# Two state-space layers: stacked float32r step-size products, a later small projection, and step sizes of the first layer grouped by function

## What is computed

```python
xp = jnp.einsum('bld,rd->blr', x, x_proj_w)           # 512 -> 16 + 16 + 16
dt = jax.nn.softplus(jnp.einsum('blr,dr->bld', dt_in, dt_proj_w) + dt_proj_b)
h = dA_t * h + dBx_t                                  # scan over 64 tokens
y = jnp.moveaxis(ys, 0, 1) + D * x
```

```python
u, gate = jnp.split(hidden_states @ W_in.T, 2, axis=-1)        # 1024 each
u = jax.nn.silu(conv4(u) + conv_b)
dt, Bm, Cm = jnp.split(u @ Wx.T, [R, R + N], axis=-1)          # 32 + 16 + 16, each rms-normalised
delta = jax.nn.softplus(dt @ Wdt.T + dt_bias)                  # 32 -> 1024
state = dA * state + (d_t * u_t)[..., None] * B_t[:, None, :]
y = (ys + u * D_param) * jax.nn.silu(gate);  return y @ W_out.T
```

## Time and profile before

| | us |
|---|---|
| median of three runs | 3992.61 (3990.76 to 3992.87) |
| the profiled execution | 3989.96 |
| its span | 3988.2 |
| busy: TensorE | 3646.0 (91%) |
| busy: VectorE | 2273.9 (57%) |
| busy: ScalarE | 1538.5 (39%) |
| busy: GpSimd | 1382.3 (35%) |
| mean granted clock of TensorE | 0.958 |
| first layer, first step-size product to scan stage | 1085.36 to 1115.41 |
| second layer, first stage | 3269.87 to 3409 |
| second layer, step sizes, group 0 | 3409.30 to 3444.32 |
| second layer, step sizes, group 1 | 3638.63 to 3672.61 |

### The profile page before, as it was taken

One profiled execution on the slowest core, in us unless ns is written; L12 is line 12 of the kernel. 1 busy time (PEld: TensorE's weight loads), 2 busy tenths in 40 slices (PEclk: granted clock), 3 DMA queues, 4 the chain that ended last, 5 costly groups with the idle time before them and its releaser, 6 DMA issues. The chain is left out here.

```text
span 3988.2 us, 74956 instructions
## 1 busy us (share of the span) xinstructions
PE 3646.0 (91%) x32236; PEld 2435.1 (61%) x32236; DVE 2273.9 (57%) x2567; ACT 1538.5 (39%) x2213; POOL 1382.3 (35%) x887
## 2 busy tenths in 40 slices
PE   6999999999768589999999999999999999686888
PEld 4555655555233456887877777788888747233334
DVE  3666666665299832444445544444445326597972
ACT  2555555555277312222222222222222103575740
POOL 3344444441189211111111111111111004496971
PEclk8999999999789899999999999999999999697999
DMA  6455555552222032111111111111111220221220
GB/s 210 126 139 141 146 142 139 141 148 52 86 67 81 22 144 68 40 48 40 39 31 47 30 48 40 38 40 40 48 40 44 78 79 1 78 90 53 90 69 21
DMA packets 225841, 301.66 MB, mean 76 GB/s; under 512 B 65328, under 2 KB 171760, under 8 KB 224224
## 3 DMA queue, kind: packets, MB, share of 16 engines
q1 hardware_dynamic: 225512, 296.88, 25.1%
HBM read 243.25 MB, written 53.10 MB: 74 GB/s over the span
## 5 line engine op out<-in xcount | busy, mean ns | idle before, releaser
L1743 POOL TENSOR_TENSOR D_ctx_lo<-D_ctx_raw,D_ctx_hi 128x1904 fp32r<-128x1904 f32 x64 | 256.1, 4003 | 1291.2 <-ACT D_ctx_hi L1737 1291.2
L762 DVE TENSOR_REDUCE A_mxc<-A_psX 128x2 f32<-128x768 f32 (+2 forms) x512 | 485.6, 985 | 207.1 <-PE A_psX L792 206.1
L1058 ACT ACTIVATE A_probs<-A_psE 128x1024 f32<-128x1024 f32 (+1 forms) x416 | 426.2, 1025 | 315.0 <-PE A_psE L1091 309.8
L1761 ACT ACTIVATE D_V<-D_psY 119x384 f32<-119x384 f32 x224 | 109.8, 490 | 842.8 <-PE D_psY L1828 842.8
L2059 ACT ACTIVATE D_probs<-D_psE 119x2048 f32<-119x2048 f32 x112 | 210.5, 1879 | 415.0 <-PE D_psE L2186 415.0
L1777 DVE TENSOR_REDUCE D_mxc<-D_psE 128x4 f32<-128x1904 f32 (+1 forms) x128 | 242.2, 1893 | 190.7 <-PE D_psE L1847 190.5
L1828 PE MATMUL D_psY<-D_wv_hi,D_ctx_hi 128*119 128x384 f32 (+1 forms) x896 | 314.7, 351 | 16.5 <-DVE D_K_lo L1772 9.0
L2104 DVE TENSOR_TENSOR D_acc<-D_acc,D_probs 119x1024 f32<-119x1024 f32 x96 | 117.6, 1225 | 353.4 <-ACT D_probs L2059 353.4
L2200 PE MATMUL D_psO<-D_probs,D_V 119*32 119x256 f32 (+1 forms) x5376 | 313.3, 381 | 0.0
L1828 PE MATMUL D_psY<-D_wv_hi,D_ctx_lo 128*119 128x384 f32 (+1 forms) x896 | 302.1, 337 | 0.0
L1828 PE MATMUL D_psY<-D_wv_lo,D_ctx_hi 128*119 128x384 f32 (+1 forms) x896 | 301.9, 337 | 0.0
(11 more groups left out here) (360 smaller groups left out, 7802.4 us busy)
## 6 DMA issues: line engine op xcount, KB each, us to landing
D_ctx_raw<-in_ctx SPq DMA_DIRECT2D x48, 952.0 KB, 5.2
A_land<-in_ctx SPq DMA_DIRECT2D x32, 768.0 KB, 6.0
A_land<-in_ctx SPq DMA_DIRECT2D x16, 1024.0 KB, 5.6
E_Bn<-bc_scratch SPq DMA_DIRECT2D x64, 256.0 KB, 3.6
E_Cn<-bc_scratch SPq DMA_DIRECT2D x64, 256.0 KB, 3.4
k_scratch<-A_Khl SPq DMA_DIRECT2D x32, 384.0 KB, 5.2
A_Kst<-k_scratch SPq DMA_DIRECT2D x64, 192.0 KB, 3.5
A_land<-in_ctx SPq DMA_DIRECT2D x16, 642.0 KB, 4.4
```

Of the source, the lines that this page charges most:

```text
L762: nc.vector.tensor_reduce(mxc[:, u % 4, :, u // 4], psX[:, x % 2, :, 0:w], axis=AX_X, op=ALU.max).then_inc(x_free, 1)
L1058: nc.scalar.activation(probs[0:KW[k], n % NPR, :, :].rearrange("p h q -> p (h q)"), psE[0:KW[k], :], ACT.Exp, scale=HD ** -0.5).then_inc(e ...
L1743: nc.gpsimd.tensor_tensor(ctx_lo[c][:, :, 0:w], ctx_raw[c][:, :, 0:w], ctx_hi[c][:, :, 0:w].bitcast(F32), ALU.subtract).then_inc(lo_done[c ...
```

## The change

- *Step sizes of the second layer.* z becomes one float32r product over 128 rows. PT is made on 128 partitions: wx, lnw and share hold the dt part three times, at rows 0, 64 and 96. ScalarE copies PT to the float32r tile PS in two halves, VectorE subtracts to get the low part in rows 96 to 127. The weights ws have in the same way high part, zeros, low part, high part. PT itself moves to a fixed place, and eu shares the space of duT.
- *Small projection two chunks behind*: x_product(c - 2) from c = 2 on, and three at the end. The last chunk's U is made by VectorE.
- *An early Ln* of the tiny eps behind the squares.
- *First layer*: the second layer's pattern: Abs from PSUM for all four chunks in ORDER, then Exp, then Ln; transposes of xpT behind the first product; du of chunks 1 and 3 on GpSimd; duT copied by ScalarE.

```diff
@@ l0_mamba, TensorE
+                    pe.wait_ge(x_out, 2)
+                    for k, c in enumerate(ORDER):
+                        if k == CN - 1:
+                            pe.wait_ge(b_out, 1)
                         for half in range(2):
-                            pe.wait_ge(x_out, 2)
-                            nc.tensor.matmul(ps[:, 2 * c + half, :], wdt[:, bass.ts(c, P)],
-                                             xpT[0:R, bass.ts(half, 512)], start=True, stop=True).then_inc(z_full, 1)
...
+                        last.then_inc(z_full, 1)
+                        if k == 0:
+                            for t in range(NPAIR):
+                                last = nc.tensor.transpose(ps[:, 2 * ORDER[-1], RN * t:RN * t + RN],
+                                                           xpT[:, bass.ts(t, P)], consts["ident"][0:RN, 0:RN])
+                            last.then_inc(b_full, 1)
@@ l0_mamba, GpSimd
                     ffn_weights.prepare(pool)
+                    for k, c in enumerate(ORDER):
+                        if c not in B_ON_PE:
+                            pool.wait_ge(delta_made, k + 1)
+                            nc.gpsimd.tensor_tensor(du[:, c, :], delta[:, c, :], XnT[:, c, :], ALU.mult)
@@ l1_mamba, loads
-            nc.sync.dma_start(wx[:, :, :], a["L1_attn_Wx"]).then_inc(wx_in, 16)
+            nc.sync.dma_start(wx[:, :, 0:RN], a["L1_attn_Wx"]).then_inc(wx_in, 16)
+            for row in COPIES[1:]:
+                nc.sync.dma_start(wx[:, :, row:row + R], a["L1_attn_Wx"][:, :, 0:R]).then_inc(wx_in, 16)
+                nc.sync.dma_start(lnw[row:row + R, :], a["L1_attn_dt_ln_w"].rearrange("o n -> n o")).then_inc(wx_in, 16)
...
+            for row in COPIES:
+                nc.sync.dma_start(wdt[row:row + R, :], a["L1_attn_Wdt"]).then_inc(wdt_in, 16)
@@ l1_mamba, TensorE
-                        if c == 1:
-                            pe.wait_ge(wx_in, 64)
-                        x_product(c - 1)
+                        if c == 2:
+                            pe.wait_ge(wx_in, 16 * 8)
+                        if c >= 2:
+                            x_product(c - 2)
+                    x_product(C - 2)
                     x_product(C - 1)
@@ l1_mamba, ScalarE
                         norm.out(act, t)
+                    act.wait_ge(wdt_in, 48)
+                    act.wait_ge(wdt_zero, 1)
+                    nc.scalar.activation(ws[:, :], wdt[:, :], ACT.Copy).then_inc(ws_hi, 1)
                     act.wait_ge(padded, 1)
...
                     act.wait_ge(eps_made, 1)
+                    nc.scalar.activation(early[:, :], eps[:, :], ACT.Ln)
                     act.wait_ge(ms_full, 2)
...
+                    for half in range(2):
+                        act.wait_ge(pt_made, half + 1)
+                        nc.scalar.activation(PS[:, bass.ts(half, 512)], PT[:, bass.ts(half, 512)], ACT.Copy
+                                             ).then_inc(ps_hi, 1)
@@ l1_mamba, GpSimd
+                    pool.wait_ge(ws_hi, 1)
+                    link(nc.gpsimd.tensor_tensor(ws[RN:RN + R, :], wdt[RN:RN + R, :], ws[RN:RN + R, :].bitcast(F32),
+                                                 ALU.subtract))
-                    for c in range(C):
+                    for c in range(C - 1):
@@ l1_mamba, VectorE
+                    dve.wait_ge(sig_u, C)
+                    nc.vector.tensor_tensor(U[:, C - 1, :], U[:, C - 1, :], eu[:, (C - 1) % 2, :], ALU.mult
+                                            ).then_inc(silu_last, 1)
...
-                    nc.vector.scalar_tensor_tensor(PT[:, :], psx[0:RN, :], lnw[:, 0:1], rms, ALU.mult, ALU.mult)
+                    for half in range(2):
+                        nc.vector.scalar_tensor_tensor(PT[:, bass.ts(half, 512)], psx[:, bass.ts(half, 512)],
+                                                       lnw[:, 0:1], rms[:, bass.ts(half, 512)], ALU.mult, ALU.mult
+                                                       ).then_inc(pt_made, 1)
+                    for half in range(2):
+                        dve.wait_ge(ps_hi, half + 1)
+                        rest = slice(RN + R, P)
+                        nc.vector.tensor_tensor(PS[rest, bass.ts(half, 512)], PT[rest, bass.ts(half, 512)],
+                                                PS[rest, bass.ts(half, 512)].bitcast(F32), ALU.subtract)
@@ l1_mamba, TensorE, step sizes
-                                                            wdt[:, bass.ts(CG * g + c, P)],
-                                                            PT[0:R, bass.ts(half, 512)], start=True, stop=True)
+                                                            ws[:, bass.ts(CG * g + c, P)],
+                                                            PS[:, bass.ts(half, 512)], start=True, stop=True)
```

More of the change, by code:

```diff
@@ new lines, in _ @@
+                    for k, c in enumerate(ORDER):
+                        dve.wait_ge(z_made, k + 1)
+                        dve.wait_ge(ln_made, k + 1)
+                        nc.vector.tensor_tensor(delta[:, c, :], delta[:, c, :], du[:, c, :], ALU.add
+                                                ).then_inc(delta_made, 1)
+                        if c in B_ON_PE:
+                            dve.wait_ge(delta_made, k + 1)
+                            nc.vector.tensor_tensor(du[:, c, :], delta[:, c, :], XnT[:, c, :], ALU.mult
+                                                    ).then_inc(du_made, 1)
@@ L2368, in x_product @@
                     def x_product(c):
-                        pe.wait_ge(silu_u, c + 1)
+                        if c < C - 1:
+                            pe.wait_ge(silu_u, c + 1)
+                        else:
+                            pe.wait_ge(silu_last, 1)
                         for half in range(2):
-                            last = nc.tensor.matmul(psx[0:RN, bass.ts(half, 512)], wx[:, c, :],
+                            last = nc.tensor.matmul(psx[:, bass.ts(half, 512)], wx[:, c, :],
                                                     U[:, c, bass.ts(half, 512)], start=(c == 0), stop=(c == C - 1))
@@ L2397, in _ @@
                         pe.wait_ge(sq_made, half + 1)
-                        nc.tensor.matmul(ps[0:RN, 1, bass.ts(half, 512)], share[:, :], sq[:, bass.ts(half, 512)],
+                        nc.tensor.matmul(ps[:, 1, bass.ts(half, 512)], share[:, :], sq[:, bass.ts(half, 512)],
                                          start=True, stop=True).then_inc(ms_full, 1)
@@ L2462, in _ @@
                     nc.gpsimd.memset(eps[:, :], RMS_EPS).then_inc(eps_made, 1)
+                    pool.wait_ge(eps_made, 1)
+                    nc.gpsimd.memset(wdt[R:RN, :], 0.0).then_inc(wdt_zero, 1)
+                    pool.wait_ge(wdt_zero, 1)
                     norm.power_of(pool, range(0, NPAIR // 2))
@@ L2468, in _ @@
                     link(nc.gpsimd.memset(share[0:R, :], 0.0))
-                    link(nc.gpsimd.memset(share[0:R, 0:R], 1.0 / R))
+                    for row in COPIES:
+                        link(nc.gpsimd.memset(share[0:R, row:row + R], 1.0 / R))
                     link(nc.gpsimd.memset(share[R:RN, :], 0.0))
```

104 lines of the change are left out of this document (53 added, 51 removed).

## The result

| | before | after |
|---|---|---|
| median, us (runs) | 3992.74 (4) | 3964.47 (4) |
| lowest to highest | 3990.76 to 3994.68 | 3962.47 to 3968.65 |
| profiled execution / its span | 3989.96 / 3988.2 | 3962.47 / 3960.7 |
| mean granted clock | 0.958 | 0.963 |

The account below looks back on a forecast made before the run. TensorE, busy for 91% of the span, was taken to bound the kernel. Terms -9.8 - 9.7 - 4.3 - 4.4 + 1.5 + 3.2 = -23.5 us took 3992.61 to 3969.1 us, range 3965 to 3976.

Parts of the forecast that it names:

- Step sizes: Second layer's two step-size stages: stacked float32r products bring the last Abs earlier, minus 9.8 us (group 0) and 9.7 (group 1).
- Rival 3: Second layer's step sizes: stacked 128-row products run as slowly as the old 3.41 us, 19.5 us go, 3988.6; chance 0.03.
- Two chunks behind: Second layer's first stage: 2.2 us of TensorE loss goes, plus 0.2 in each of five periods; last chunk drained 3.2 earlier.
- Last U on VectorE: End of second layer's first stage: U ends at 3393.9 instead of 3395.05, 1.1 us earlier; TensorE then idles 1.1 us.
- Clock and early Ln: End of second layer's first stage: clock stays full, table load follows the squares, Ln 4.2 us after projection's start; minus 4.4.
- rival 1: The clock falls after all before the last small projection; costs 3.1 us, giving 3972.2; chance 0.27.
- PT and PS: End of second layer's first stage: PT in halves, ScalarE's copies and VectorE's subtraction take 2.8 us instead of 1.27; plus 1.5.
- First layer: First layer's step-size stage: regrouped code starts the next stage at 1118.6 instead of 1115.41; plus 3.2 us, bounds 2.3 to 3.5.
- at 1098.95: First layer's step-size stage: the last product comes 1.08 us later than 1097.87, because the eight transposes stand behind product 0.
- hides nothing new: First layer's step-size stage: GpSimd's weight preparation ends before du is ready in both kernels, so it has no effect.
- Loads: Second layer's first stage: added short-run loads take 5.4 us more, wdt lands near 3294.8, copy ends before drain 0; cost 0.
- The range: Whole kernel: 3965 to 3976 us, covering the forecast, rival 1 and most of two lesser rivals.

Follow-up runs that it names:

- z_float32: Changed kernel with the second layer's stacked 128-row step-size product read as float32 instead of float32r; 3975.92 us (one run).
- lag1: Changed kernel with the small projection one chunk behind again instead of two; 3971.03 us (4 runs), ratio 0.9946.
- last_u_pool: Changed kernel with the last chunk's U made by GpSimd again instead of VectorE; 3964.86 us (one run).
- l0_old: Changed kernel with the first layer as before the change (step sizes by chunk, seven table loads); 3962.31 us (5 runs), ratio 0.9929.
- gap_longer: Changed kernel with two more VectorE passes (times 1.0) behind the last U; 3963.46 us (one run).
- l0_t_late: Changed kernel with the first layer's eight transposes and VectorE's copy of them moved behind the fourth product; 3965.10 us (one run).
- l0_rows128: Changed kernel with the first layer's wdt and xpT padded with zero rows to 128, products still float32; 3960.14 us (5 runs), ratio 0.992.
- after_same: The changed kernel unaltered, run again as a base on the same chip as later experiments; 3962.66 us (5 runs), ratio 0.993.

## Why the prediction was right or wrong

The four changed stretches gained 3.6 us more than forecast: 1.6 in the first layer, 1.9 in the second layer's first stage and 0.1 in the groups.

- *Step sizes, -9.8 and -9.7.* Measured -9.5 and -10.1, with the last Abs at the forecast places, and with the products of group 0 at the half clock that the prediction gave them. Right, in size and mechanism. Rival 3, "as slowly as the old 3.41 us", was mis-sized: it had no room for a clock that rises, and in z_float32, where it does, 10.3 us go and not 19.5.
- *Two chunks behind, -3.2.* This step failed by size. Chunk 7's last large group starts 118.13 us into the stage in before and 113.30 in after, 4.8 earlier. The 2.2 us were right; the other term, 0.2 us in each of five periods, is 0.51 (13.16 to 12.65), 2.6 us instead of 1.0 and above its bound of 2.1. That bound came from 13.16 - 10.9 - 1.83, which counted the projection and the group behind it as if they didn't overlap. After runs both in 12.65. lag1 shows that 0.36 of the 0.51 are the lag; of before's loss the timeline puts 0.28 us ahead of the projection, waiting for GpSimd's U (1.19 us from group to projection, 0.91 in after), and 0.25 behind it (2.89 to the second group against 2.64). lag1 has 1.16 to 1.19 and 2.75; why before loses another 0.14 behind a projection with fewer columns was not tried.
- *Last U on VectorE, -1.1.* TensorE idled 1.41 us and not 1.1, and last_u_pool gives 1.36 for the start. It was worth more than that in the one execution of last_u_pool: with the longer gap the clock fell, and the stage was 3.06 longer in all.
- *Clock and early Ln, -4.4.* Ln starts 4.03 us after the projection instead of 4.2, -4.6. The clock stayed up in all thirteen executions with the 1.4 us gap, so rival 1's chance of 0.27 looks too high for this gap. Of the three with about twice the gap, two let it fall.
- *PT and PS, +1.5.* From Ln to the next stage 5.55 us before, 7.12 after: +1.6.
- *First layer, +3.2.* The sign was right and l0_old shows it, the size failed in this execution: +1.6, below the bounds of 2.3 to 3.5. The step that failed is the last product "at 1098.95". It kept the clock of before, which fell 1.6 us after the first product. In after it held for 4.5 us, through product 0, the transposes (0.69 us, not 1.08) and the second product, and the last Abs came at 11.27 us instead of 13.59. In the executions where the clock fell sooner it came at 12.2 to 13.8, and the stretch took 32.9 to 33.8 us, +2.8 to +3.8. The forecast described these. The tail behind the last Abs was 20.3 us, not 19.66, and the sentence that GpSimd's preparation "hides nothing new" was wrong. Where VectorE's first sum took 1.23 us (gap_longer, lag1, z_float32, l0_t_late), the tail was 20.01; what the preparation added to that sum came on top of it (1.56 us and 20.34 in after, 2.48 and 21.27 in last_u_pool).
- *Loads, 0.* Right, and wdt was in well before 3301, but not by the forecast's way. SyncE issued its three loads 19.3 us into the stage instead of 15.6, behind the issues of wx and its two copies (1.74, 1.89 and 0.55 us) and of more lnw, and each landed within 2.3 to 2.5 us, so the last was in by about 3295.7, just as the copy began. The forecast had 5.4 us of transfer more; how much of the 3.7 us of delay is the short runs was not tried.
- *The range.* Its width rested on three runs within 2.1 us. In the thirteen profiled executions without an edit ahead of the first layer's stage, the stretches that no edit touches add up to 3743.4 to 3754.1 us; 8.9 of these 10.7 us lie ahead of that stage's first product (1081.23 to 1090.08). Code that is the same varies by more than the distance from the forecast to the low end. With the right terms (-27.1) the forecast would have been 3965.5, still within 0.5 us of that end.

## What to carry to other kernels

Price a TensorE product with few rows at the clock it will have, and try zero rows up to 128 before a new number format: in z_float32 128 rows brought the clock up and kept 9.3 of the 19.6 us of the stacked product, and in l0_rows128 112 rows of zeros took the first layer's last Abs from 11.3 to 8.0 us. When a stage gets faster on one engine, look at what the engine behind it shares with GpSimd's background work: of 2.7 us freed on ScalarE 0.6 arrived, and all of them once the weights' loads were issued earlier. And take the spread of a forecast from stretches that nothing touches, over several executions, not from the medians of a few runs.

## What was not expected of the hardware

- Float32 products with 16 rows let the granted clock fall from 1.00 to 0.50 while TensorE was busy without a break; where it fell differed between executions of the same code (second Abs at 4.55 to 6.99 us after the first product). With 128 rows, most of them zeros, it stayed at 1.00 (l0_rows128), and in float32 it rose (z_float32). The 128-row float32r products of after's group 0 were over in 5.5 us and had 0.50 throughout.
- The same projection of the first layer ahead of this (L1237), the same code behind the same idle 1.27 us, took 8.73 us in after with the clock partly at 0.50 and 7.04 us in after_same with the clock at 1.00. This is one source of the spread between executions. It also goes with the place of the fall: in the eight executions of this stage the second Abs came at 4.55 or 4.56 us where the projection had taken 8.73 to 9.23, at 5.40 to 6.01 where it had taken 7.04, and at 6.99 where it had taken 9.59.
- Behind idle gaps of 2.56 and 2.85 us the clock fell to half within the next product, behind one of 2.77 us it did not.
